# Attention layers of a fused four-stage kernel: rings of five, eight and six turned probability tiles in place of four, and small VectorE chains moved to other steps

## The reference

```python
# L0: 16 heads of 32, full 512 keys, cosine attention
qn = q / max(norm(q), 1e-12) * exp(min(scale_mul_log, log(100)))
kn = k / max(norm(k), 1e-12)
p = softmax(qn @ kn.T + attn_bias)
x = x + (p @ v @ Wproj.T + bproj) * gamma1
# L1: 16 heads of 32, keys and values from a latent of 128, rope,
#     a window of 64 keys within past blocks, and every 64th key
x = x + softmax(where(mask, -inf, q @ k.T / sqrt(32))) @ v @ Wo.T
# L2: 8 heads of 64 on one k and v, rope, full 512 keys
x = x + softmax(q @ k.T / 8) @ v @ Wo.T
```

## Time and profile before

| what | before |
|---|---|
| runs | 2754.55, 2747.24, 2753.22 us; median 2753.22 |
| the profiled execution's own time, its span | 2748.22 us, 2746.4 us |
| mean granted TensorE clock | 0.915 of full speed |
| busy share of PE, DVE, ACT, POOL over the span | 87%, 57%, 47%, 33% |

### The profile page before, as it was taken

How to read it: one execution, slowest core, us unless ns; L and a number is a source line. 1 busy time by engine, 2 the same in 40 slices (tenths; PEclk the granted TensorE clock), 3 DMA queues, 4 the chain that set the end, 5 groups by cost and what they waited for, 6 DMA issues and landing times. The chain is left out here.

```text
span 2746.4 us, 47159 instructions
## 1 busy us (share of the span) xinstructions
PE 2384.2 (87%) x15672; PEld 1933.7 (70%) x15672; DVE 1564.9 (57%) x4470; ACT 1281.2 (47%) x3188; POOL 902.4 (33%) x988
## 2 busy tenths in 40 slices
PE   6789899988699998688888778989899999996777
PEld 4677787776578886466666566777688888885565
DVE  5877777786644343646457367457643333334866
ACT  4677777767311111567667456556521111112453
POOL 0334343434476766123223123224111221111321
PEclk8899999999899999687887789999999999997988
DMA  6000000000200100110000000000100000001000
GB/s 259 1 2 2 9 3 9 2 9 17 77 31 20 42 0 32 44 63 2 1 1 1 20 24 1 1 0 1 47 24 24 23 23 23 0 0 50 8 24 31
DMA packets 17089, 65.24 MB, mean 24 GB/s; under 512 B 3293, under 2 KB 4061, under 8 KB 12277
## 3 DMA queue, kind: packets, MB, share of 16 engines
q1 hardware_dynamic: 16884, 62.70, 6.4%
HBM read 57.42 MB, written 5.28 MB: 23 GB/s over the span
## 5 line engine op out<-in xcount | busy, mean ns | idle before, releaser
L1979 POOL TENSOR_TENSOR l2m_hidl<-l2m_hid,l2m_hidh 128x512 fp32r<-128x512 f32 x64 | 100.8, 1576 | 445.6 <-DVE l2m_hidh L1949 445.6
L1844 ACT ACTIVATE l2m_gate<-l2m_psG 128x512 f32<-128x512 f32 x64 | 38.3, 598 | 437.4 <-PE l2m_psU L1775 436.5
L1123 ACT ACTIVATE l0a_prob<-l0a_prob,l0a_nmin 128x512 f32<-128x512 f32 x256 | 185.3, 724 | 91.4 <-DVE l0a_nmin L1406 90.8
L1601 POOL TENSOR_TENSOR l0a_prob<-l0a_prob,l0a_rinv 128x512 f32<-128x512 f32 x64 | 66.9, 1045 | 449.8 <-DVE l0a_rinv L1413 449.8
L1944 DVE TENSOR_TENSOR l2m_hid<-l2m_gate,l2m_psU 128x512 f32<-128x512 f32 x64 | 44.0, 687 | 282.2 <-ACT l2m_gate L1844 282.2
L1135 ACT ACTIVATE l0a_PT<-l0a_psT 128x512 f32<-128x512 f32 x256 | 152.4, 598 | 72.6 <-PE l0a_psO L976 52.1
L1406 DVE CUSTOM_DVE_ANT_0 l0a_prob<-l0a_psS,l0a_mask 128x512 f32<-128x512 f32 x256 | 174.8, 688 | 6.3 <-PE l0a_psS L934 6.0
L808 PE MATMUL l0a_psA<-res_l0a_wh,res_hTh 128*128 128x128 f32 (+1 forms) x512 | 154.3, 301 | 19.6 <-ACT l0a_raw L1032 6.5
L1999 POOL TENSOR_TENSOR res_X<-res_X,l0m_share 128x512 f32<-128x512 f32 x128 | 162.9, 1305 | 24.0 <-DVE l0m_share L1933 22.9
L1848 ACT ACTIVATE l0m_hid<-l0m_psG,l0m_b1c 128x512 f32<-128x512 f32 x64 | 43.9, 690 | 262.9 <-PE l0m_psG L1775 262.9
L955 PE MATMUL l0a_psT<-res_ident,l0a_prob 128*128 128x128 f32 x1024 | 161.1, 281 | 3.5 <-ACT l0a_PT L1135 3.4
(11 more groups left out here) (410 smaller groups left out, 7658.1 us busy)
## 6 DMA issues: line engine op xcount, KB each, us to landing
res_l2m_stage<-in_l2m_w SPq DMA_DIRECT2D x8, 1536.0 KB, 6.5
res_l0m_stage<-in_l0m_w SPq DMA_DIRECT2D x8, 1024.0 KB, 4.8
cond_w<-in_wmod SPq DMA_DIRECT2D x6, 1024.0 KB, 16.2
res_X<-in_x SPq DMA_DIRECT2D x4, 1024.0 KB, 12.4
l1a_wmod<-in_wmod SPq DMA_DIRECT2D x4, 1024.0 KB, 5.7
out<-res_X SPq DMA_DIRECT2D x16, 256.0 KB, 2.0
l_stage<-in_l_w SPq DMA_DIRECT2D x3, 1024.0 KB, 7.0
cond_stage<-in_l0a_w SPq DMA_DIRECT2D x3, 768.0 KB, 13.7
```

The costliest lines, as they stand in the source:

```text
L1123: act.activation(prob[:, n % NP, 0:w], src[:, 0:w], ACT.Exp, bias=nmin[:, n % NP:n % NP + 1], scale=-1.0, accum_out=ssum[:, n % NP:n % NP ...
L1601: op = pool.tensor_tensor(x, x, r.to_broadcast([P, w]), ALU.mult)
L1979: pool.tensor_tensor(hidl[:, s % 2, m, :], hid[:, m, :], f32(hidh[:, s % 2, m, :]), ALU.subtract).then_inc(hl_done, 1)
```

## The change

- `PT` is a ring of `RING` tiles: five in L0 (four as before and a tile `PT4`), eight in L1 (each 256 wide in place of 512) and six in L2. `slot(m)` gives the tile's place, `turned(m)` the tile, and `held_until(m)` the weighing that has to be over before the slot is written: in L0 for j = 0 the one a unit earlier than before, in L1 for all four j, in L2 for four tiles of six.
- In L0 the guess and first Newton step go to s = 6, the second and the factors to s = 7, the scaling to s = 9, in every group. The five parts of `inverse_deviations` go to the steps 0, 1, 4, 5 and 5 behind the start (`SMALL_AT`); L2 starts them one step later in the first batch and three earlier in the last. The rows' factors for the norms (`norm_factors`) come one step later.
- L2 has two tiles `xn` in place of four, and the transposes of its third and fourth row tile stand one step later.
- `bG` goes: `G` holds first gamma times bias, which GpSimd adds, and is then loaded again with gamma for DVE. In the queue of SP the load of the MLP's first weights comes ahead of the last of these loads.

Line numbers in the changed kernel's attention are 27 higher from L792 on (L808 is L835, L955 is L982, L976 is L1003, L1123 is L1150, L1135 is L1162, L1406 is L1433).

```diff
--- before.py
+++ after.py
@@ -479,7 +479,7 @@
     CL = 1
     PROJ0 = 0
     NORM0 = 7 if L is L0 else LAG + 1
-    NORM_T = (0, 1, 3, 4) if L is L0 else (0, 1, 2, 3)
+    NORM_T = (0, 1, 2, 3) if L is L1 else (0, 1, 3, 4)
     VCP = max(LAG + 2, PROJ0 + NT + 3)
     GS = 4 * NT
     is0, is1, is2 = L is L0, L is L1, L is L2
@@ -506,7 +506,9 @@
             wh = S.room(R, "wh", [P, WCOLS], wh_at, F32R)
             wl = S.room(R, "wl", [P, WCOLS], wl_at, F32R)
         hTh, hTl = R.hTh, R.hTl
-        XS = 2 if is0 else NT
+        XS = NT if is1 else 2
+
+        RING = 5 if is0 else 8 if is1 else 6
         xn = S.sb("xn", [P, XS, C])
 
         NR = 2 if is0 else NG
@@ -522,7 +524,10 @@
         V = S.sb("V", [P, VS, NT, L.VW])
         prob = S.sb("prob", [P, NP, T])
         tail_at = wl_at + 4 * WCOLS
-        PT = S.sb("PT", [P, 4, T]) if is2 else S.room(R, "PT", [P, 4, T], tail_at)
+        PT_shape = [P, 4 if is0 else RING, 2 * P if is1 else T]
+        PT = S.sb("PT", PT_shape) if is2 else S.room(R, "PT", PT_shape, tail_at)
+        if is0:
+            PT4 = S.sb("PT4", [P, 1, T])
         oTh = S.room(R, "oTh", [P, NK, T], tail_at + 8 * KB, F32R) if is1 else S.sb("oTh", [P, NK, T], F32R)
         oTl = S.sb("oTl", [P, NK, T], F32R)
         late = [S.at(f"late{i}", [P, NK * T], F32, nc.sbuf_base - (16 - 8 * i) * KB) for i in range(2)]
@@ -547,8 +552,8 @@
         beat = S.sb("beat", [P, NP])
         if is0:
             qb = S.sb("qb", [P, C])
+
             G = S.sb("G", [P, C])
-            bG = S.sb("bG", [P, C])
             nrm = S.sb("nrm", [P, 4, 4 * 8])
             sq = xn[:].rearrange("p r c -> p (r c)").rearrange("p (t w) -> p t w", w=QKW)
         if L.rope:
@@ -621,9 +626,12 @@
 
 
         FIRST_TILE = (B - 1) * NT if is2 else NT
-        FIRST_AT = NT * NT + 1 if is2 else 2
+
+
+        FIRST_AT = NT * NT + 2 if is2 else 2
         LAST_TILE = (B - 1) * NT
-        LAST_AT = 9 if is2 else 14
+        LAST_AT = 6 if is2 else 14
+        SMALL_AT = {0: (0,), 1: (1,), 4: (2,), 5: (3, 4)}
 
         def norm_step(n, more):
 
@@ -637,6 +645,23 @@
 
             n = n % NTILE
             return NS - 2 if n == NTILE - 1 and NTILE % NS else n % NS
+
+        def slot(m):
+
+
+
+            m = m % NTILE
+            return m % RING + (2 if is2 and m >= NTILE - 2 else 0)
+
+        def turned(m):
+
+            return PT4[:, 0, :] if is0 and slot(m) == 4 else PT[:, slot(m), :]
+
+        def held_until(m):
+
+
+            last = next(k for k in range(m - 1, m - NTILE, -1) if slot(k) == slot(m))
+            return last // 4 + 1
 
         def since(n):
 
@@ -767,18 +792,20 @@
                     for b in range(B):
                         if b > 0:
                             sp.wait_ge(out_done, NT * b)
+                        sp.dma_start(G[:], bcast_rows(D["gam_rows"][1, b])).then_inc(g_in, 16)
+                        if b == B - 1:
+                            sp.wait_ge(v_mm, 2 * NG * B)
+                            sp.wait_ge(proj_done, NT * NG * B)
+                            sp.dma_start(pre_stage[:, 0], D[nxt.weights][0]).then_inc(pre_in, 16)
+                        sp.wait_ge(xg_done, b + 1)
                         sp.dma_start(G[:], bcast_rows(D["gam_rows"][0, b])).then_inc(g_in, 16)
-                        sp.dma_start(bG[:], bcast_rows(D["gam_rows"][1, b])).then_inc(g_in, 16)
-                    sp.wait_ge(v_mm, 2 * NG * B)
-                    sp.wait_ge(proj_done, NT * NG * B)
                 if is1:
                     sp.wait_ge(mod_mm, len(GROUPS))
                     for i in range(2):
                         sp.dma_start(pre_stage[:, i], D[nxt.weights][:, i * WCH:(i + 1) * WCH]).then_inc(pre_in, 16)
                     sp.wait_ge(pre_in, 32)
-                else:
-                    if is2:
-                        sp.wait_ge(w_lo, len(chunks))
+                if is2:
+                    sp.wait_ge(w_lo, len(chunks))
                     sp.dma_start(pre_stage[:, 0], D[nxt.weights][0]).then_inc(pre_in, 16)
 
             @block.tensor
@@ -974,7 +1001,7 @@
                             else:
                                 v, rows = V[:, hg % VS, qt if is1 else c, v0:v0 + HD], P
                             mm = pe.matmul(psO[o][row:row + HD, qt * P:(qt + 1) * P],
-                                           v, PT[0:rows, j, c * P:(c + 1) * P],
+                                           v, turned(4 * u + j)[0:rows, c * P:(c + 1) * P],
                                            start=(c == 0), stop=(c == nk - 1))
                     mm.then_inc(pv_done, 1)
 
@@ -1130,9 +1157,9 @@
                     if is0 and first and m == 0:
                         act.wait_ge(R.tab_out, 32)
                     act.wait_ge(pT_mm, b * NTILE + (m + 1))
-                    if not (first and u == 0):
-                        act.wait_ge(pv_done, b * U + u)
-                    act.activation(PT[:, j, 0:w], psT[m % 2][:, 0:w], ACT.Copy).then_inc(pT_done, 1)
+                    if not (first and held_until(m) <= 0):
+                        act.wait_ge(pv_done, b * U + held_until(m))
+                    act.activation(turned(m)[:, 0:w], psT[m % 2][:, 0:w], ACT.Copy).then_inc(pT_done, 1)
 
                 def o_copy(b, hg):
 
@@ -1210,8 +1237,8 @@
                     if 0 <= i < last - first:
                         v.drain()
                         tile_stats(first + i)
-                    else:
-                        inverse_deviations(v, R, i - (last - first), first, last, eps, rms)
+                    for part in SMALL_AT.get(i - (last - first), ()):
+                        inverse_deviations(v, R, part, first, last, eps, rms)
 
                 def norm_factors(b):
 
@@ -1426,6 +1453,7 @@
                     if is0:
                         if t == 0:
                             v.wait_ge(xg_done, bo + 1)
+                            v.wait_ge(g_in, 32 * (bo + 1))
                         v.tensor_tensor(xn[:, t % XS, :], ps[:], G[:], ALU.mult)
                         v.drain()
                         v.tensor_tensor(x, x, xn[:, t % XS, :], ALU.add).then_inc(out_done, 1)
@@ -1442,14 +1470,13 @@
                             qk_squares(hg)
                         if p == 3:
                             qk_norms()
-                        if p == 4:
+                        if s == 6:
                             rsqrt_guess(v, *qk_tiles)
                             rsqrt_newton(v, *qk_tiles)
-                        if p == 5:
+                        if s == 7:
                             rsqrt_newton(v, *qk_tiles)
-                        if p == 6:
                             qk_factors(hg)
-                        if p == 7:
+                        if s == 9:
                             qk_scale(hg)
                     elif is2 and hg < NG:
                         if s in (1, 2):
@@ -1506,7 +1533,7 @@
                         if not more:
                             statistics(n - LAST_AT, 0, LAST_TILE, nxt.eps, nxt.rms)
                         bn, x = b + 1 if more else B, norm_step(n, more)
-                        if x == -2:
+                        if x == -1:
                             norm_factors(bn)
                         if x - 2 in NORM_T:
                             norm_split(bn, NORM_T.index(x - 2))
@@ -1604,9 +1631,9 @@
                             op.then_inc(p_done, 1)
                         if is0 and u >= U - 4:
                             if u == U - 4:
-                                pool.wait_ge(g_in, 32 * (b + 1))
+                                pool.wait_ge(g_in, 32 * b + 16)
                             x = R.X[:, b * NT + (u - (U - 4)), :]
-                            add = pool.tensor_tensor(x, x, bG[:], ALU.add)
+                            add = pool.tensor_tensor(x, x, G[:], ALU.add)
                             if u == U - 1:
                                 add.then_inc(xg_done, 1)
 
```

## The result

| | before | change |
|---|---|---|
| median of 11 runs each | 2748.92 us | 2735.56 us |
| lowest and highest | 2746.82, 2754.55 | 2722.75, 2741.40 |
| ratio, 95% interval | | 0.9946 (0.9935 to 0.9958) |
| profiled execution, its span | 2748.22, 2746.4 | 2725.21, 2723.4 |

By the ratio the change is 0.54% faster, 15 us of 2749; the medians lie 13 us apart. The forecast was 17 us. The changed kernel spreads over 19 us, the one before over 8. Its profiled execution is one of its fastest, so the two profiles differ by 23 us, 10 more than the medians do. The mean granted clock differs with it: 0.925 in the profiled execution, 0.918 in the one of 2741.4 us. The length of a single profile is therefore no measure of a part worth 3 us.

The account below looks back on a forecast made before the run. PE was taken to bound all three windows, with gains only from its 167 idle us. Terms -6 - 4 - 1 - 4 + 1.5 - 3.5 + 0 = -17 from the median 2753.2 gave 2736 us, range 2718 to 2755.

Parts of the forecast that it names:

- Rings: ACT's copies into `PT` wait less for the weighing: -6 us in L0, -4 in L1, -1 in L2.
- ACT's wait under 30 us: Sign of being right: ACT's wait for the weighing at the copy, 111 us before, falls under 30 in all.
- L1's copies at 20 us or less: Sign of being right: PE's waits at the probabilities' transposes in L1 fall from 24 us to about 20 or less.
- half of 0.31 for each of 29: L1: PE stood 0.31 us behind one late copy; half taken for each of ACT's 29 waits, -4 us.
- Inverse norms in L0: L0's small DVE chain, moved to steps 6 and 7 where GpSimd has finished: -4 us, bounds 0 and -6.8.
- inverse deviations, -3.5: L2's first and last batch: parts moved to steps after GpSimd's unit, 2 x 1.7 us won, bounds 0 and -4.7.
- Scaling: L0, 12 groups: moved from step 7 to 9, into GpSimd's products; costs +1.5 us, bounds 0 and +5.
- slower rival: L0's scaling holds GpSimd's products up in 12 groups, transposes come late; about 2763 us, chance 0.10.
- Norms in L2: Third and fourth row tile's transposes a step later, k's wait only changes name: 0 us, bounds -1 and +4.5.
- Gamma rows: G's second load lands 3.6 us before DVE reads it: 0 us, at most 4 x 1 us.
- PE's idle time stays at 167 us: Sign of being wrong: PE's idle time in the three windows unchanged within a few us, so nothing reaches the path.
- larger rival: All bounds reached in L0, L1 and L2, PE perhaps keeping more of its clock; about 2722 us, chance 0.14.

## Why the prediction was right, point by point

The time was right, 2736 against 2735.6, and partly by luck, in two ways. The forecast started from a median of three executions, 2753.2, and eleven give 2748.9, so the gain was 13 to 15 us and not 17. And of its terms the chains were too small and L2's norms, put at nothing, cost 7 to 9 us; the two errors cancel.

- **Rings, -11.** Measured 11 to 13 for all three waits, 13 for L0 and L1 with L2 as before. In L0 the lengths give 6, as forecast, and the mechanism stood as told: it is not ACT's wait that is won but the one bank that ACT empties earlier. Of the signs named in advance, ACT's wait under 30 us came true (6.4); L1's copies at 20 us or less did not (24.4). L1 became 5 us shorter, as long as the forecast's 4, but not at the waits from which "half of 0.31 for each of 29" was worked out; where, stays open.
- **Inverse norms in L0, -4, and inverse deviations, -3.5.** The chains alone gave 11 to 13, and 5 to 7 beside the rings. The step that failed is that only L2's inverse deviations were costed; those of L0 and L1 moved too, for which the lengths give about 4 and 6 us. In L0 a 1.02 us product of `res_rs` in step 16, near 106 us of the trace of before, stood behind the same reciprocals. L93's median fell from 1016 to 181 ns, as said, but the group at full clock lost nothing to the old place. The gain, of the norms and the scaling together, is seen in the first batch: its first two groups took 73.4 to 73.7 us in the four profiles with the old chain and 69.5 to 70.3 in the ten others, with the wait of 2.84 us for a minimum near 120 us down to 1.97.
- **L2's inverse deviations, -3.5, and their steps.** The two waits of the earlier trace rows went, but the waits for the minimum in L2 rose to 17.0 us where about 12 was the sign, and the statistics that start three steps earlier cost 3.0 us in the last batch, which no step of the sum had. The prediction gave the start of the statistics as the steps of the parts: they follow four and twelve steps later (22, 23, 26, 27 and 18, 19, 22, 23). That they all have n % 4 of 2 or 3 holds.
- **Scaling, +1.5.** Its median rose from 1.225 to 1.442 us, half of the 0.4 allowed. The sum missed what its old place cost: 0.55 us in the second group of the second and of the third batch, where it stood ahead of a residual product. The slower rival was right in its mechanism and wrong in its price. In 12 units of L0, and in 9 of the 12 groups where the scaling moved, it held one of GpSimd's products up by 1.0 us, as the rival says; the sign named for it, the median of 192 products, could not show that (0.693). But no wait of PE in L0 names these products, as the prediction's objection has it: the unit's tiles have two steps until they are transposed. The Trainium skill's "SBUF — State Buffer", section "Who interferes with whom", would have one engine stand for the other's whole instruction. The trace agrees for the 32-wide chain (0.18 against 1.02 us), and for the 1024-wide scaling on GpSimd's side: the product issued behind it took 1.65 us in place of 0.69, while the scaling, issued into a product already running, lost 0.3.
- **Norms in L2, 0, bounds -1 and +4.5.** Measured +7 to +9, from three sides (one of them with L2's ring taken back too). This is the term that failed most. It counted ACT's work ahead of k's transposes, and that wait grew by 0.45 us only, to 1.98, which was a sign named for 'wrong' (over 1.5). It missed that two row tiles make PE wait for VectorE, that the weighing comes earlier than its copies, and that the weighing then ran at 1.2 GHz.
- **Gamma rows, 0.** No wait for G shows in the profile after; the last addition ended at 666.1 and DVE read G at 673.5. No run tested it alone.
- **"PE's idle time stays at 167 us" as the sign of no gain** was a bad sign: it stayed at 167 and the kernel was faster. The claim behind it, that the change can win only out of those 167 us, failed too: PE's busy time fell by 19 us for the same matmuls, part of it clock. The sum had no term for the clock; it stood only in the larger rival.
